# A decoder layer on one core: VectorE takes the operand ranges as they land, four projections begin ahead of the scale, an early table load, 36 warm-up matmuls, a new order of units

## The reference

```python
def reference(x, ctx, mask, ...):
    q, k, v = split_heads(x @ Wq + bq), split_heads(x @ Wk + bk), split_heads(x @ Wv + bv)
    att = softmax(where(causal, q @ k.T / 4, -inf))
    x = layernorm(x + (att @ v) @ Wo + bo)
    Q, K, V = heads(x, w_q), heads(ctx, w_k), heads(ctx, w_v)
    x = layernorm(x + softmax(where(mask, -1e9, Q @ K.T / 4)) @ V @ w_o.T)
    gate = silu(bitlinear(x, w_gate)); up = bitlinear(x, w_up)
    return layernorm(x + bitlinear(gate * up, w_down))
# bitlinear: rows of x rounded to 8 bits of their own scale, weights rounded to -1, 0, 1 of one scale
```

## Time and profile before

| | us |
|---|---|
| median of three runs | 849.23 (847.72 to 849.62) |
| the profiled execution, its time | 847.58 |
| its span in the profile | 845.5 |
| TensorE busy | 797.8 (94%) |
| VectorE busy | 687.9 (81%) |
| ScalarE busy | 574.6 (68%) |
| GpSimd busy | 342.9 (41%) |

### The profile page before, as it was taken

The page is one execution under the profiler, slowest core; times in us unless marked ns, Lnnn a source line. Parts: engine busy times, 40 slices in busy tenths (PEclk is TensorE's granted clock), DMA queues, the critical chain, the costliest instruction groups (busy, mean ns, idle before and its releaser), DMA issues.

```text
span 845.5 us, 20914 instructions
## 1 busy us (share of the span) xinstructions
PE 797.8 (94%) x7816; PEld 395.7 (47%) x7816; DVE 687.9 (81%) x1261; ACT 574.6 (68%) x751; POOL 342.9 (41%) x582
## 2 busy tenths in 40 slices
PE   8889999999999989999999999999999999999997
PEld 6534345344564434534454344543545443445645
DVE  4899998948998699887999689974899848836698
ACT  1277856467965588655885679866597579864595
POOL 3832454344333055431544245442425403552344
PEclk9999999999999999999999999999999999999999
DMA  7422102100211011100131020101110001010001
GB/s 233 94 83 58 46 20 72 42 21 3 49 47 58 1 41 38 26 26 10 40 87 26 11 79 2 39 11 29 39 52 2 8 1 52 2 51 1 2 2 52
DMA packets 37189, 32.90 MB, mean 39 GB/s; under 512 B 9828, under 2 KB 33252, under 8 KB 37092
## 3 DMA queue, kind: packets, MB, share of 16 engines
q1 hardware_dynamic: 33844, 28.93, 12.2%
q0 software_dynamic: 1536, 1.58, 0.8%
q10 hardware_dynamic: 1712, 1.05, 0.5%
HBM read 14.55 MB, written 4.19 MB: 22 GB/s over the span
## 4 chain that ended last, share of the span: by engine, by line
PE 64%; DVE 20%; ACT 6%; issue 5%; POOL 2%; ACTq 1%; DMA 0%; SPq 0%; POOLq 0%; DVEq 0%
PE ps L1031 12%; DVE shift L1376 11%; PE ps L826 8%; PE ps L1016 7%; PE ps L994 6%; PE ps L839 5%; PE ps L965 3%; PE ps L790 3%; PE ps L977 3%; PE ps L892 3%; PE ps L922 2%; PE ps L917 2%; PE ps L815 2%; PE ps L934 2%; ACT probs L1137 2%
## 5 line engine op out<-in xcount | busy, mean ns | idle before, releaser
L1376 DVE TENSOR_REDUCE shift<-ps 128x2 f32<-128x1024 f32 (+2 forms) x320 | 343.9, 1111 | 39.6 <-PE ps L994 19.4
L1137 ACT ACTIVATE probs<-ps 128x1024 f32<-128x1024 f32 (+3 forms) x384 | 294.2, 811 | 103.9 <-PE ps L1016 101.4
L1031 PE MATMUL ps<-probs,v_aug 128*32 128x512 f32 (+3 forms) x1536 | 157.5, 499 | 0.1
L705 POOL TENSOR_SCALAR_AFFINE_SELECT probs<-probs 128x512 f32<-128x512 f32 x128 | 80.7, 640 | 163.8 <-ACT probs L1137 163.0
L994 PE MATMUL ps<-k_stack,q_stack 48*128 48x512 f16 (+3 forms) x768 | 114.6, 330 | 13.2 <-DVE shift L1376 4.8
L1016 PE MATMUL ps<-q_stack,k_stack 49*128 49x512 f16 (+3 forms) x768 | 116.0, 328 | 10.4 <-DVE shift L1376 4.9
L1016 PEld LDWEIGHTS ps<-q_stack,k_stack 49*128 49x128 f16 x768 | 37.6, 93 | 112.9 <-ACT probs L1137 37.9
L994 PEld LDWEIGHTS ps<-k_stack,q_stack 48*128 48x128 f16 x768 | 40.3, 93 | 97.2 <-DVE shift L1376 34.5
L1000 PE MATMUL ps<-causal,pick_h 64*128 64x64 bf16 x1024 | 53.3, 190 | 0.0
L1078 ACT ACTIVATE full<-ps,bias_scaled,kq_scale 128x512 f32<-128x512 f32 x32 | 25.0, 780 | 41.5 <-PE ps L839 32.3
L1000 PEld LDWEIGHTS ps<-causal,pick_h 64*128 64x128 bf16 x1024 | 46.4, 96 | 14.4 <-issue 0.5
(11 more groups left out here) (205 smaller groups left out, 1361.0 us busy)
## 6 DMA issues: line engine op xcount, KB each, us to landing
q_stack<-part_sb SPq DMA_DIRECT2D x168, 32.0 KB, 2.0
k_stack<-part_sb SPq DMA_DIRECT2D x144, 32.0 KB, 2.0
xT<-in_x_cols SPq DMA_DIRECT2D x8, 512.0 KB, 4.5
xt<-in_x SPq DMA_DIRECT2D x8, 512.0 KB, 4.1
out_x<-xt SPq DMA_DIRECT2D x7, 512.0 KB, 3.5
q_stack<-shiftT SPq DMA_DIRECT2D x128, 1.0 KB
k_stack<-part_sb POOLq DMA_DIRECT2D x48, 32.0 KB, 2.0
region<-in_w_gate SPq DMA_DIRECT2D x4, 256.0 KB, 4.2
```

Source lines behind the costliest of these rows:

```text
L705: pool.affine_select(out=blk, in_=blk, compare_op=ALU.is_ge, fill=0.0, base=0, pattern=[[0, HG], [1, P]], channel_multiplier=-1).then_inc( ...
L1031: mm = pe.matmul(ps[DV * i:DV * (i + 1), SUM_BANK, off:BANK], v_aug[:, kb, at:at + DV], probs_of(b, n)[:, i, :], start=first, stop=last)
L1137: act.activation(probs_of(b, n)[:, 2 * p:2 * p + 2, :], pair(u)[:, :, 0:BANK - off], ACT.Exp, scale=exp_scale).then_inc(probs_ready, 1)
L1376: dve.tensor_reduce(to[:, :, pairs[0]:pairs[-1] + 1, qb % TH], pair(u)[:, :, 0:len(pairs) * w].rearrange("p j (h w) -> p j h w", w=w), AX. ...
```

## The change

- `tops` of batch 0 now also makes `w_top` (w_k, then the first half of xT, w_q, then the second half) and `b_sum`, each behind the wait for its own load; the wait for `consts_ready` goes to `take_bound` of batch 0 and, on PE, to directly ahead of the bound's products.
- `begun` is the list of those of the first four `kq` units whose bank nobody used before. With the new order these are all four (banks 0, 1, 2, 3). PE issues their d = 0 products behind the warm-up transposes and ahead of its wait for `tops_ready`; the d = 1 products stay at the units' place.
- ScalarE issues one 128x1 activation (`first_out`) behind its three loads, when `round_c` is written (`pool_ready` 5).
- 36 transposes in place of 70.
- `ORDER` is new, with 59 stirs in place of 70. Read unit by unit: all eleven stirs taken out are those behind the last used matmul; 44 stand ahead of the end of the self-attention and 15 behind it in both. Of PE's 1408 other units 835 keep their place in PE's own sequence, the mean displacement is 0.7 places and the largest 13; on DVE it is 609 of 694, at most 4 places. Silu and Exp alternate at the same 13 points. In batch 0 the first feed-forward loads stand behind the third `max` (five of them) in place of ahead of `tops`; `kq4` stands ahead of the first `max`; the two first `abs` units (sums over feed-forward weights, ACT) follow one another; the second `x_half` of batch 1 stands behind the shift load of group (0, 3) on SP where it stood ahead of it, `tops` of batch 1 keeps its place among the maxima. In the last part six stirs stand between the last-but-one and the last `up` tile.

```diff
-STIRS = 70
+STIRS = 59
+WARM_UP = 36
@@
-    "ffrr6r0sr6sz0ffr0r6wr0ssffgr6m01m23ggm45r6gm23m01m45r6m01r2m45m01m23r6m01m45a23a01aw6a23z4w4a01m23aa56om01m4"
-    "5m23w6wssa01fffoffaa45a01aa23a45agm01m23m45a01m23a01wz6m45am01om23m45r6a23m01m45oa23aa01z6xom23m45a01gfr6m23"
...
-    "u6u0pvvpu2u1u6u3ppvp45p0p6upz3z3uz3uuv23u6u4pppp01p5p2p6v3v4v5z2uuuuu23v6pz4pppp45v0v1vvvvv0v1p6p45vu23p0p6v"
-    "vvv23pu0ptu6uv23v1v6vutz0z0z6z6vz6z6z6z6z6z6z6t"
+    "rr6r0sr1sr2r3r6wgr1ssgr6m01m23m45gfffffr6gm23m01m45m23r6z4m45m23m01r6m23m45a01a23am01fz6a45w6w2m01a45om45am2"
+    "3sffw6fsga01a45aa01a23aa45a01m23om45m23aa01a45am01z6m45wwom01m23m45r6a23m01a45aoom23z6a01a45z6m01o23gm45r6m2"
...
+    "6u2u4u3ppppu6u5vp01p4p6vuuuuu5v23ppppp01p6u5p4p2v6v5v3v4uupppuuu01pp56v2v3vz4vz4z4z4z4vvv4z3v0p1p45u23vp6vp4"
+    "pu5vvv23u4upv01v6v0vuvttt"
@@
+        first_out = sb("first_out", [P, 1])
@@ tensor
+            begun = [n for n in range(SLOTS) if not find["kq", 0, n].before]
+
+            def project(u, ds):
+
+                t, e, h = pieces[u.idx]
+                if u.b == 0:
+                    pe.wait_ge(kq_loaded[1 - t], 16)
+                pe.wait_ge(x_loaded[h], 16 * (u.b + 1))
+                for d in ds:
+                    mm = pe.matmul(ps[:, u.bank, :], (wk, wq)[t][:, d, e * P:(e + 1) * P],
+                                   xT[:, h, d, :], start=(d == 0), stop=(d == CC - 1))
+                return mm
@@
                 if kind == "kq":
-                    t, e, h = pieces[u.idx]
-                    if b == 0 and u.idx < 2:
-                        pe.wait_ge(kq_loaded[1 - t], 16)
-                    pe.wait_ge(x_loaded[h], 16 * (b + 1))
-                    for d in range(CC):
-                        mm = pe.matmul(ps[:, k, :], (wk, wq)[t][:, d, e * P:(e + 1) * P],
-                                       xT[:, h, d, :], start=(d == 0), stop=(d == CC - 1))
+                    mm = project(u, [d for d in range(CC) if b > 0 or d > 0 or u.idx not in begun])
                 elif kind == "bound":
                     if b == 0:
-                        stir(u, 70)
+                        stir(u, WARM_UP)
+                        for n in begun:
+                            project(find["kq", 0, n], [0])
+                        pe.wait_ge(consts_ready, 1)
                     pe.wait_ge(tops_ready, b + 1)
@@ scalar
+            act.wait_ge(pool_ready, 5)
+            act.activation(first_out[:], round_c[:], ACT.Identity, bias=round_c[:, 0:1])
@@ vector, tops
                 for h in range(QC):
+                    if b == 0:
+                        dve.wait_ge(kq_loaded[1 - h], 16)
+                        link(dve.tensor_reduce(w_top[:, :, h], (wk, wq)[h][:], AX.X, ALU.max, apply_absolute_value=True))
                     dve.wait_ge(x_loaded[h], 16 * (b + 1))
                     link(dve.tensor_reduce(x_top[:, h, :], xT[:, h, :, :], AX.X, ALU.max, apply_absolute_value=True))
                 link(dve.tensor_tensor(x_top[:, QC, :], x_top[:, 0, :], x_top[:, 1, :], ALU.max))
+                for t, bias in enumerate((bk_c, bq_c)) if b == 0 else ():
+                    dve.wait_ge(bias_loaded[1 - t], 16)
+                    link(dve.tensor_reduce(b_sum[:, t:t + 1], bias[:], AX.X, ALU.add, apply_absolute_value=True))
@@ vector, take_bound
+                if b == 0:
+                    dve.wait_ge(consts_ready, 1)
@@ vector, ahead of the loop over the units
-            dve.wait_ge(consts_ready, 1)
-            for t, bias in enumerate((bk_c, bq_c)):
-                dve.wait_ge(bias_loaded[1 - t], 16)
-                link(dve.tensor_reduce(b_sum[:, t:t + 1], bias[:], AX.X, ALU.add, apply_absolute_value=True))
-            for t, w in enumerate((wk, wq)):
-                dve.wait_ge(kq_loaded[1 - t], 16)
-                link(dve.tensor_reduce(w_top[:, :, t], w[:], AX.X, ALU.max, apply_absolute_value=True))
```

More of the change, by code:

```diff
@@ new lines @@
+    "r4m23a56aa01oa45am23rm01oa45oom23m45a01az6z6om23m01wea45r6a23aa01o45om23a01az6z6m01m45a23oooa23m01m45roggr6b"
+    "ra01o45m23om45p01z6z6a23em45a01p6gm01m45a23p6z4a45a23pm01r6m23m45m01oa23opp45cm01m23z6m01m45p6m01a23m45p6pp2"
+    "p3p4p5paa01oa23aa01p4z6p6p5p2a01aa34oa01m45aa23a01p6op25a01rr4rp23p05m23r4p23p01p56m23z4z4p23a45p01z6z6m45m2"
+    "3p01oom45op6a45m23m01p6a23o45opm23a45a01grr6m45m01oa45pa23paom01a45z6pa23roppam45a01a23r6aa01m45p23om01ga45p"
+    "6am23m45op0p1p6p2m45m01p3p6p2p4p3pa56a01aoom23or4a01a56pppp2p3z4o01paa45om01a23aa45pr6ga45ppp23p0aa45p6z1xa0"
@@ new lines @@
+    "1pm23aa45opppp01p6p4p5a23pz6z6aa01a23bam45r6pppa23a45gm01op23m45p6m01m23p45goop6p4aa01o23a56pom23pp01a45oooo"
+    "tm01m23m45p6m23a01p4pa23a01o56oa23z4z4m01a23m45opa23a01op45m23m01m23m45p6m23m01m45p6poaa01p6p2p3p4a01paa56oa"
+    "01am23a56ea01ap4p5a01a23p6p4om01a56p4oooa01p35xrr2r0p45p02rr6bp45p01p23o45op23p45a01om23p45z6m01m23a45p6a23m"
+    "45m01p6a45pm23a01roa45aopm01a45m23m01gga45oam23pa45a01az6a45a01aa23m45a01ppaooa23m01m45pr6m01a23am45p01m23oo"
+    "m45a01p6m23m01p4p5m23p6p4p5m01m23p6p4p5ra01ap6o23pr4a23a01am56ppporgp4p0a23a56aooooppm23ppm01p45r6a23o45p0p1"
@@ new lines @@
+    "pa45aa23oa45aa01a23apm45m01ppp23p6p4gp5a23a01ooooppm23m45ppp01p6o23om01p45p6m23a01p4ppp6a01a23p5p4p01m23op6a"
+    "23m45a01rp6pa01a45a23r6m45m01opm45aa23om01a23ap45orm01m23a45p6tm01m45m23p6pp4a01ap5p2a01a34p6paa01m45om23a01"
+    "p6a45ooop2p3a01p6a45a23o01p6om01p25m01om01p23p05r4grp23p01p56m23ga01p45p23m01m45p23oa01m23p6ea23m01m45p6a01a"
+    "pm23pa45r6m45a01oaa23a01am45oa01a23aa45pa01m23aoopm45pprbm01a23r6a45m23p01om45m23m01gp6r4xm23m01ogp6p4p5p2p6"
+    "am34m01p5p2p3p4a56o01ooa01aa23a45appppp6p0pa23a45pr6m23ppp01p4p6pooaa23m45a01r6oo01ppcpp23p4p6p5aa23a01poaa2"
@@ new lines @@
+    "3a45aa01m23pm45oxppp01p6m23m45p01p6m23a01p4ppp56ta23ooom01m45p6a01m23p4a23o01a56oa01ppm23a45om01a45ra23oaa01"
+    "a45om23p01m45m23m01p6m23m45m01p6paa23p4p5a01p6p2epaa34om45a01ap6p2p3a01a45op6a01m23a45op6m01oor2p35o01r2p45p"
+    "02rr6p45p01rp23m45op23a01p45a23m01p45om01a23a45p6m23m45gp0a23a45r6aga23pm45om01m23a45ppoaa01a45aa01a23aa45m0"
+    "1a23aoa45m01a23aopppm45m23m01rr6rm23a45m01op45m23ooa01p6m45o23p0p1m45m23p6p0ap1p4m23m56p0p1a23p4oa56aa01a23a"
+    "oa45a01appppp6p2oooa45a01apm23pppr6o45p01p2p3a45oa01aa23a45pppgpp01p6p2p3pra45ogooom01pppp23p6o45m01bom45p23"
```

50 lines of the change are left out of this document (15 added, 35 removed).

## The result

The changed kernel takes 839.71 us (median of six runs, 838.97 to 841.68), the kernel before 849.42 in the same rounds (six runs, 847.7 to 852.86): a ratio of 0.9885, with a 95% interval of 0.986 to 0.9911. The forecast was 845.2, with 841.5 as its lower end. The direction is right, and so are several of the times that the forecast named; the size is 2.4 times too small: 9.7 us gained where 4.05 were forecast. The profiled execution of the changed kernel took 839.96 us; its span is 838.2, that is 7.3 less than the 845.5 before, and TensorE's share is still 94% (page, part 1; compare rows 1).

The account below looks back on a forecast made before the run. VectorE was taken to be full from 30 to 60 us, TensorE later, with a chain at the start; bound 2.75 plus table load 1.30 gave 4.05 us, so 849.23 - 4.05 = 845.2 us, range 841.5 to 849.3.

Parts of the forecast that it names:

- VectorE takes the tops as operands land: At the start, VectorE's reductions begin as each load lands; `v_top` ends at 10.9 instead of 14.45, 3.55 us taken alone.
- 36 warm-ups and four halves: TensorE ahead of the bound: warm-ups until 8.25, four half projections 3.44 us, bound at 11.75, 2.75 us earlier (2.0 to 3.55).
- What the halves buy: 3.44 us less TensorE work behind the bound, off the first `full`'s path; third and fourth `full` follow without waits.
- Early table load: ScalarE loads its table while idle, ahead of the bound, taking 1.30 us off the first `full` at no cost.
- Rival D: The table is loaded again at the first `full`, so that term fails: gain 2.75 us, time 846.5; chance 0.06.
- From the first `full` to the first maximum: Steps as before, last piece landing in 4.00 us (0.5 either way); first maximum from 28.86 to about 24.9.
- VectorE's full stretch keeps what the start gains: From 30 to 60 us VectorE is full, so each microsecond by which this stretch begins earlier is kept.
- Rival B: A longer TensorE gap ahead of the first maximum halves the clock, costing up to 1.7 us: gain 2.35, 846.9; chance 0.12.
- The stirs taken out: Matmuls behind TensorE's last used one; removing them is worth 0, since the last store's landing ends the span.
- The order of the rest: Units reordered beyond the start: put at 0, with 2 us either way.
- Rival C: `kq4`'s 1.7 us of TensorE count and the order removes waits in the middle: gain 7 us, time 842.2; chance 0.15.
- Rival E: Slower: TensorE's dips at ScalarE's 13 Silu/Exp changes grow; 0.31 us each eats the gain, 0.45 gives 851.0; chance 0.12.

Follow-up runs that it names:

- new order alone: Kernel before with the new order of units and 59 stirs, its start unchanged (70 warm-ups, late tops, table load at the first `full`): 847.22 us, ratio 0.9963.
- new start alone: Changed kernel with the order of before and its 70 stirs, only the first unit begun: 845.13 us, ratio 0.9948 to the kernel before.
- old tail: Changed kernel with the order of before behind the self-attention, its eleven last stirs included: 842.98 us, ratio 0.9913 to the kernel before.
- stirs in the tail: Changed kernel with the eleven last stirs put back (70 in all): 839.67 us, ratio 0.9878 to the kernel before.
- five more idle units: Changed kernel with five more stirs on TensorE, two ahead of the first scores and three behind them: 839.66 us, ratio 0.9877 to the kernel before.
- old rest: Changed kernel with the order of before from about 100 us on: 844.28 us, ratio 0.994 to the kernel before.

## Why the prediction was wrong, step by step

The sum of 4.05 failed at three terms. The landing of the last piece was carried over at 4.00 and was 2.18. The bound was put at 11.75 and came at 11.07. The new order was put at 0 and brings about 1 to 2.5 us by itself and some more together with the new start.

To add up, I take the stretches out of the spans, at 1.4 us each (1.2 to 1.8 above). A second measure is near it: over 51 runs of the kernel before, six with a mean granted clock of 0.996 average 847.0 us, 27 with 0.990 average 850.0 and eight with 0.988 average 851.9. A step of 0.002 is 845.5 x 0.002 / 0.5 = 3.4 us at half clock, and costs (851.9 - 847.0) / 4 = 1.23.

| kernel | span | stretches where work was left | span less 1.4 each | gain |
|---|---|---|---|---|
| before | 845.5 | 2 | 842.7 | |
| new order alone | 846.2 | 4 | 840.6 | 2.1 |
| new start alone | 843.1 | 5 | 836.1 | 6.6 |
| both, old order from 100 us | 840.2 | 3 | 836.0 | 6.7 |
| both, old tail | 841.6 | 5 | 834.6 | 8.1 |
| changed | 838.2 | 3 | 834.0 | 8.7 |
| changed, stirs in the tail | 838.0 | 3 | 833.8 | 8.9 |

By this account the two parts add up: 6.6 and 2.1 to 8.7. But it rests on one profile for each kernel and on a rounded price. Runs with the same mean granted clock, 0.990, say something else:

| kernel | runs | mean us | gain |
|---|---|---|---|
| before | 27 | 850.0 | |
| new order alone | 3 | 847.9 | 2.1 |
| new start alone | 4 | 845.0 | 5.0 |
| changed | 2 | 841.5 | 8.5 |

Here 1.4 us remain that only the two together bring. The clock at the end, which falls without the last stirs and costs nothing, lowers the mean clock of the changed kernel and of the new order alone by about 0.002. Set beside runs of the kernel before at 0.992 they gain 7.5 and 1.1, and the rest is 1.4 again. These groups are small too. A cause is at hand, since only the new order gives the banks for three of the four begun halves, but no run has the new start and order with one half begun, so it isn't shown. The rest to the 9.7 of the medians is that the kernel before usually has more stretches than the changed one: the median of its 51 mean clocks is 0.990, that of the changed kernel's six 0.993.

- *VectorE takes the tops as operands land.* Right. `w_top` begins at 6.23 (forecast 6.2), `v_top` ends at 10.92 (10.9), 3.53 earlier (3.55).
- *36 warm-ups and four halves.* Mis-sized by 0.7 us in the profiled execution. From rows 4 I had the warm-ups last to about 8.25, because the transposes of the kernel before came closer together only at about 7.1 us. In the profile of the changed kernel they do at 5.5, the first half begins at 7.46, and the bound waits for VectorE at 11.07, not 11.75. The term was 3.44, not 2.75, near the upper end that I gave (3.55). With the change at 7.2, as in the run with five more idle units, the bound comes at 11.71 and the working holds. What I missed is that this moment differs between executions (4.6 to 7.2 us over all profiles); the 0.7 is luck of the execution.
- *What the halves buy.* Wrong by what it left out. I said that the 3.44 us of TensorE's work taken from behind the bound aren't on the path of the first `full`, and gave the waits that they spare the third and fourth no price. Without them the first `full` is 0.55 later, TensorE becomes what the first maximum waits for, 1.78 later, and the end 1.38 with one stretch less.
- *Early table load.* Right: 1.30 at the first `full` for a forecast of 1.30 (1.37 with the 0.07 that the biases come later). Rival D has fallen.
- *From the first `full` to the first maximum.* The term of the start that was mis-sized most. SP's first move waits for the second `full`, not for the first as I wrote; it made no difference, since the steps up to the last issue took 6.02 us for 6.03. But I carried over the landing of 4.00 with 0.5 either way, and it was 2.18. And I costed the move of the feed-forward loads at 0 to 0.5 of loss, looking only at what they run beside in their new place: put back ahead of the moves, they make the landing 3.50. That doesn't explain the 4.00 of the kernel before, whose loads were through by 19.8 us; its cause stays open. The first maximum came 6.58 earlier instead of 4.0. VectorE gave 0.87 of it back up to the first transpose: one `v_aug` now stands ahead of it, and one `shift_h` takes 0.71 instead of 0.21.
- *VectorE's full stretch keeps what the start gains.* Right in the runs that test it (70 warm-ups: 3.75 late at the first maximum, 4.82 at the end; old rest: 4.3 to 4.5 kept for 586 us), wrong for the profiled fill, where VectorE was idle 4.2 us behind a TensorE at half clock.
- *Rival B, the clock.* The mechanism is real and its price was well put (up to 1.7 for a stretch, measured 1.2 to 1.8), its trigger isn't: no stretch followed the longer gap ahead of the first maximum in this profile (1.70 us of wait, not 3.6), and by the mean clocks of its runs (0.990 to 0.994; 0.986 to 0.996 before) the changed kernel has no more of them in general than the kernel before.
- *The stirs taken out*: 0 within 0.2, as forecast.
- *The order of the rest.* Mis-sized: 0 within 2 forecast, alone it brings 2.5 in the medians, and 1.1 to 2.1 beside runs of about the same mean clock. In the profiles it shows as 1.9 us in the last stage and about 1 in the middle (5.37 at the 32nd transpose, with one stretch more than before at equal work: 6.8; 5.7 at the third). Of the losses that I had allowed for, the tops of batch 1 show none (no wait ahead of them at 102.70), and the last stage gains as a whole. Which of the moved units make the gain I haven't shown.
- *Rival C, more than the start* (842.2, 0.15) is the nearest in size, and was still 2.5 us short. Its mechanism isn't shown: no run isolates the 1.7 of `kq4`, and 2.5 us of what came beyond the 4.05 are the bound's and the landing's. I had argued against it from TensorE's 94%. But its busy share is 94% in the changed kernel too, of a span 7.3 us shorter, with 12.4 us less busy time: 4.97 of it are the last stirs and 4.50 the warm-ups (10.54 us for 70, 6.04 for 36), products that nobody used. A busy share with such filler in it didn't bound what was left.
- *Rival E* (slower at the changes of Silu and Exp): no sign of it. The changed kernel's lead stays between 3.0 and 6.2 us from the first Silu (208 us before) to the 32nd transpose and is 5.37 there, 7.3 at the end.
- *The range.* Its lower end, 841.5, took most of C and nothing beyond it. The misses (0.7 at the bound, 1.8 at the landing, 1 to 2.5 for the order and what it gives the start) point the same way, and I had set each near its cautious end.

## What to carry to other kernels

Cost a load not only where it goes but where it leaves. A latency read once is no constant: take the shortest and the longest landing of that kind in the trace as bounds (1.9 us stood in the profile of the kernel before, beside the 4.00), and look whether the traffic that is blamed for the long one was still there. Before a move is credited to a cause, put the cause back by itself in both kernels. When an engine is taken off the path, look one step further down for where it would be late next; work done in its idle time may be what keeps it off. And before explaining a loss by a stretch at half clock, look at a second execution of the same work, and compare runs with the same mean clock: here the stretches alone move 1 to 3 us about, and the moment at which TensorE comes to full speed moves the bound by 0.6.

## What the runs showed of the hardware

- TensorE's granted clock fell to 0.50 for 3.4, 6.8 or 10.2 us at a time in every profile of this kernel, two to seven times 3.4 us in an execution, also where it was busy throughout (23 to 27 us above: 4.00 of 4.00 us busy). I found no gap that decides it. A stretch of 3.4 us costs 1.2 to 1.8 us where TensorE or its consumers have no slack, and nothing behind the last product.
- At the start the transposes come every 0.21 us and later every 0.11. The change comes between 4.6 and 7.2 us after the span's start, at different times in executions of the same instructions, while the clock column of the windows shows 1.00 throughout.
- A 32 KB move between SBUF tiles landed in a median of 2.0 us in the changed kernel and 3.2 with six 256 KB loads running into the moves. It also took 3 to 4 us in the kernel before, 4 us after such loads had landed.
- One small activation on an idle ScalarE took the table load out of the first large one, for 0.29 us of its own. At the fourteen table loads of the kernel before the next activation starts 0.01 to 0.03 us behind the load.
